# Shorter waits at the seams of a two-pass expert layer: rows counted at run time, tables and loads moved

## What is computed

```python
def _ln_c(v): return (v - v.mean(1)) / sqrt(v.var(1) + 1e-6)      # over channels, shortened
# attention in windows of 8 x 8 tokens
q, k, v = windows(wq @ xn + bq), windows(wk @ xn + bk), windows(wv @ xn + bv)
x = x + wo @ merge(softmax(q k^T / sqrt(128)) v) + bo             # xn = _ln_c(x)
# experts: E = 16, the two best of each token
t = to_tokens(x)
xt = _ln_t(t)
top_vals, top_idx = top_k(xt @ wg, 2)
w = softmax(top_vals)
for e in range(16):
    h = silu(xt @ w0[e]) * (xt @ w1[e])                           # 128 -> 256
    out = out + dense_w[..., e] * (h @ wo[e])                     # 256 -> 128
x = from_tokens(t + out)
```

## Time and profile before

| | us |
|---|---|
| median of 3 runs | 437.34 (437.17 to 438.48) |
| the profiled execution | 439.65 |
| its span, first to last instruction | 437.6 |

### The profile page before, as it was taken

How to read it: one execution, slowest core, us unless ns; L and a number is a source line. 1 busy time by engine, 2 the same in 40 slices (tenths; PEclk the granted TensorE clock), 3 DMA queues, 4 the chain that set the end, 5 groups by cost and what they waited for, 6 DMA issues and landing times.

```text
span 437.6 us, 9336 instructions
## 1 busy us (share of the span) xinstructions
PE 374.4 (86%) x2581; PEld 307.4 (70%) x2581; DVE 303.2 (69%) x1101; ACT 268.2 (61%) x778; POOL 234.7 (54%) x286
## 2 busy tenths in 40 slices
PE   4698887888876489999999999679999999999373
PEld 4476676666755348888888888458888888888242
DVE  4578999999986865766767667326767676676163
ACT  2688888887883136666666666336666666666100
POOL 7000055665575577776666666606666676666400
PEclk9999999999997558999999999969999999999886
DMA  7999999740110176777655532265454454421299
GB/s 231 365 350 197 160 152 149 223 149 26 39 51 31 49 158 161 200 210 203 178 140 141 141 117 86 99 175 162 141 145 131 127 152 133 140 64 49 99 351 348
DMA packets 56151, 68.07 MB, mean 156 GB/s; under 512 B 7588, under 2 KB 44328, under 8 KB 55800
## 3 DMA queue, kind: packets, MB, share of 16 engines
q1 hardware_dynamic: 45136, 43.13, 42.6%
q0 software_dynamic: 8368, 20.03, 13.3%
q10 hardware_dynamic: 2600, 4.33, 2.6%
HBM read 37.03 MB, written 36.65 MB: 168 GB/s over the span
## 4 chain that ended last, share of the span: by engine, by line
PE 62%; DVE 21%; DMA 7%; ACT 4%; SPq 3%; issue 2%; POOL 0%; POOLq 0%; DVEq 0%
PE bank L657 9%; PE bank L660 9%; PE bank L658 9%; PE bank L676 8%; PE bank L677 8%; PE bank L649 4%; PE bank L666 4%; PE bank L665 4%; DMA w_hi<-token_sums 3%; DMA w<-in_L_ffn_w 2%; DVE x_sb L1070 2%; DVE st L1016 2%; DVE st L1007 2%; SPq L345 2%; PE bank L492 2%
## 5 line engine op out<-in xcount | busy, mean ns | idle before, releaser
L1215 DVE SCALAR_TENSOR_TENSOR hid<-bank,late,sil 128x256 f32<-128x256 f32 x158 | 76.4, 484 | 73.6 <-ACT sil L841 72.4
L436 POOL DMA_INDIRECT token_sums<-late x79 | 76.5, 968 | 51.5 <-DVE late L1226 48.4
L841 ACT ACTIVATE sil<-bank,late 128x256 f32<-128x256 f32 x158 | 75.0, 475 | 46.0 <-PE bank L660 46.0
L432 POOL DMA_INDIRECT rows_second<-late x79 | 76.6, 970 | 35.9 <-DVE late L1224 30.7
L424 POOL DMA_INDIRECT rows_first<-rows,slot x64 | 63.5, 992 | 38.8 <-issue 16.8
L847 ACT COPY hT<-bank 128x256 f32<-128x256 f32 x158 | 59.1, 374 | 32.3 <-PE bank L666 31.3
L657 PE MATMUL bank<-w_hi,x_hi 128*128 x158 | 77.6, 491 | 1.1 <-ACT x_hi L836 1.1
L676 PEld LDWEIGHTS bank<-w_sb,hT 128*128 128x128 f32 x316 | 48.2, 190 | 29.2 <-issue 28.7
L660 PE MATMUL bank<-w_hi,x_lo 128*128 x158 | 64.3, 407 | 0.0
L676 PE MATMUL bank<-w_sb,hT 128*128 x316 | 61.8, 277 | 2.2 <-ACT hT L847 2.2
L658 PE MATMUL bank<-w,x_hi 128*128 x158 | 63.5, 402 | 0.0
(11 more groups left out here) (181 smaller groups left out, 663.3 us busy)
## 6 DMA issues: line engine op xcount, KB each, us to landing
late<-rows_second SPq DMA_DIRECT2D x79, 129.5 KB, 2.3
late<-rows_first SPq DMA_DIRECT2D x79, 66.5 KB, 2.5
w<-in_L_ffn_w SPq DMA_DIRECT2D x4, 1024.0 KB, 11.2
w_hi<-token_sums SPq DMA_DIRECT2D x16, 256.0 KB, 6.3
out<-x_sb ACTq DMA_DIRECT2D x16, 256.0 KB, 7.1
rows_second<-nobody_second SPq DMA_DIRECT2D x16, 129.5 KB
nobody_first<-late SPq DMA_DIRECT2D x1, 2061.5 KB, 21.4
x_sb<-in_x SPq DMA_DIRECT2D x1, 2048.0 KB, 13.6
```

The lines of the kernel that those rows point to most:

```text
L432: pool.indirect_dma_start(out=xs2_dram, out_offset=bass.IndirectOffsetOnAxis(ap=xg[:, u, 0:1].bitcast(I32), axis=0), in_=xg[:, u, TOK:TOK ...
L436: pool.indirect_dma_start(out=s_dram, out_offset=bass.IndirectOffsetOnAxis(ap=xg[:, u, TOK:TOK + 1].bitcast(I32), axis=0), in_=xg[:, u, YA ...
L841: act.activation(sil[:, t % 2, :], bank[2 + t % 2][:, 0:M], ACT.Silu, scale=xg[:, t % XRING, RS:RS + 1]).then_inc(sil_ok, 1)
L1215: dve.scalar_tensor_tensor(out=hid[:, t % 2, :], in0=bank[2 + t % 2][:, M:2 * M], scalar=xg[:, t % XRING, RS:RS + 1], in1=sil[:, t % 2, :] ...
```

## The change

- **Waits for tiles with rows.** TensorE adds up how many tiles of each pass have rows (`T_ALL`, one product in `tiles_upto`), VectorE turns this to a count of landings for each slot (`left_i`, three operations in `tables`), and SP reads 16 numbers (`rows_left`) and waits for these alone, ahead of pass two and ahead of the loads of the sums. The wait for all scatters comes behind these loads.
- **Room.** The sums are loaded to `rows`, `xn` and a buffer of five chunks, no longer over `w_hi`. XRING goes from 20 to 16.
- **Weights at the start** come in four quarters (EP = 4), with four experts in period 0 instead of five.
- **TensorE** does `full_ends` in period 16 behind `last_rows`, `full_rows` behind the last `last_rows`, and `tiles_upto` and `tiles_rows` one tile later. **VectorE** does `ends` and `tile_counts` behind the first tile's product, `tiles_done` and `tables` one tile later.
- **GpSimd** holds the scatters of a batch back to TensorE's and ScalarE's later periods, two by two, and does the next batch's counts ahead of the last two.

```diff
-XRING = 20
+XRING = 16
-SPLIT0 = 5
+EP = SPLIT0 = 4
...
+        def s_in(n):
+            return (s_in1[:, n, :, :] if n < TAIL1 else xn[:, n - TAIL1, :, :] if n < TAIL1 + 2
+                    else s_in2[:, n - TAIL1 - 2, :, :])
...
-            for k in range(2):
-                es = slice(k * (E // 2), (k + 1) * (E // 2))
+            for k in range(E // EP):
+                es = slice(k * EP, (k + 1) * EP)
...
+            def rows_left(k):
+                sp.wait_ge(left_ok, 1)
+                left = []
+                for u in range(XRING):
...
+                    left.append(sp.value_load(left_i[0:1, 2, k, u:u + 1], min_val=least, max_val=most))
+                for u in range(XRING):
+                    sp.wait_ge(y_out[u], left[u])
...
                     sp.wait_ge(pads2_in, (E + 1) * 16)
-                    for w in range(XRING):
-                        sp.wait_ge(y_out[w], len(range(w, TL, XRING)) * 16)
+                    rows_left(0)
...
+            rows_left(1)
+            s_v = s_dram[0:N, :].rearrange("(n p j) d -> p n j d", j=TPC, p=P)
+            for n in range(NCH):
+                sp.dma_start(s_in(n), s_v[:, n, :, :]).then_inc(s_got[n], 16)
             for u in range(XRING):
                 sp.wait_ge(y_out[u], len(range(u, TILES, XRING)) * 16)
...
                 for j in range(TB):
+                    n = min(2 * m + 7 + j // 4, NCH)
+                    if j % 2 == 0 and m == LAST:
+                        past(pool, xhi_ok, j // 2)
+                    elif j % 4 == 2:
+                        pool.wait_ge(q_ok, n)
+                    elif j == 4:
+                        pool.wait_ge(xnt_ok, n)
+                    if j == 6:
+                        counts(m + 1)
                     pool.indirect_dma_start(
...
                 token_rows(i + 2)
...
+                if i == NCH:
+                    full_ends()
...
-                if i == NCH - 1:
-                    full_ends()
             new_rows(NCH - 1)
+            last_rows(NCH - 1)
             full_rows()
-            last_rows(NCH - 1)
...
                 pe.wait_ge(nt_ok, 1)
+                pe.matmul(T_ALL, ones_f[0:E, 0:32], nt_f[:, 0, :], start=True, stop=True)
...
-                    if t == 0:
+                    if t == 1:
                         tiles_upto()
-                    if t == 1:
+                    if t == 2:
                         tiles_rows()
...
             place(LAST)
-            ends()
-            tile_counts()
...
                     if t == 0:
+                        ends()
+                        tile_counts()
+                    if t == 1:
                         tiles_done()
-                    if t == 1:
+                    if t == 2:
                         tables()
```

More of the change, by code:

```diff
@@ L181, in emit @@
         T_END, T_SUM, T_UPTO = SP_[0:32, 0:2 * E], SP_[0:E, 2 * E:2 * E + 2], SP_[0:E, 2 * E + 2:2 * E + 4]
+        T_ALL = SP_[0:32, 2 * E + 4 + 4 * TL:2 * E + 6 + 4 * TL]
         T_ROW = SP_[0:32, 2 * E + 4:2 * E + 4 + 4 * TL]
         wqk_in = sem("wqk_in"); wov_in = sem("wov_in"); b_in = sem("b_in"); wg_in = sem("wg_in")
[L186 removed]
+        e_in = [sem(f"e_in{k}") for k in range(E // EP)]; e2_in = sem("e2_in"); e_hi = sem("e_hi"); e_lo = sem("e_lo")
         x_in = [sem(f"x_in{n}") for n in range(6)]
@@ L394, in _, with counts @@
             make(pool.memset(gap0[:, :], float(CAPT)))
+            count(left_k[:, :, :], [[TL, 2], [-1, XRING]], base_=XRING - 1)
             assert made.count == CONST1
             count(iota_r[:, :, :], [[0, 2], [P, TL]])
-            for m in range(NBAT):
-                b = m % RB
+            def counts(m):
                 if m < LAST:
@@ L415, in _ @@
                                        ALU.add).then_inc(carry_ok, 1)
+            counts(0)
+            for m in range(NBAT):
+                b = m % RB
                 past(pool, sc[b], m // RB * TB * 16)
@@ L712, in _ @@
                 for j in range(TPC):
-                    mm = pe.transpose(bank[n % 2][:, tiles[j]], s_in[:, n, j, :], ident[:, :])
+                    mm = pe.transpose(bank[n % 2][:, tiles[j]], s_in(n)[:, j, :], ident[:, :])
                 mm.then_inc(ot_ps, 1)
@@ L1172, in tables @@
                 dve.wait_ge(row_ps, 1)
+                left = then(dve.tensor_tensor(left_i[:, 0, :, :], T_ALL[0:1, :].unsqueeze(2).to_broadcast([1, 2, XRING]),
+                                              left_k[:, :, :], ALU.add))
                 rest = slice(FULL, 2 * TL)
@@ L1180, in tables @@
                                   float(E - 1), float(2 * D), ALU.min, ALU.mult).then_inc(expert_ok, 1)
+                after(left)
+                left = then(dve.tensor_scalar(left_i[:, 1, :, :], left_i[:, 0, :, :], 4, None, ALU.logical_shift_right))
+                after(left)
+                dve.tensor_scalar(left_i[:, 2, :, :], left_i[:, 1, :, :], 4, None,
+                                  ALU.logical_shift_left).then_inc(left_ok, 1)
             dve.wait_ge(made_s, CONST0)
```

20 lines of the change are left out of this document (12 added, 8 removed).

## The result

| | before | after |
|---|---|---|
| median of the runs, us | 437.25 (436.90 to 438.48, 4 runs) | 412.91 (412.21 to 413.39, 4 runs) |
| span of the profiled execution, us | 437.6 | 410.8 |
| its mean granted clock of TensorE | 0.936 | 0.972 |

The ratio is 0.943, 95% interval 0.9409 to 0.9452: 24.3 us less by the medians, where 24.5 was forecast. The two profiled spans are 26.8 apart, 2.5 more.

What follows compares the result with a forecast made beforehand. The prediction saw TensorE gapless inside the passes, with time to win at five seams where it stands still. Terms 2.0 + 4.0 - 0.2 + 0 + 7.7 + 11.0 = 24.5 off 437.34 gave 412.8 us, range 408.8 to 419.5.

Steps and rivals of the forecast that it cites:

- Start, 2.0 forecast: Kernel start: weights in quarters bring the queries 2.3 us earlier, less 0.3 for the fifth cast; gain 2.0 us.
- End of the attention stage, 4.0: End of attention: two VectorE waits go (2.45 us) and TensorE's clock stays up (0.94 and 0.57); gain 4.0 us.
- Tables, -0.2: Tile tables one tile later: same work, still at the slow clock, plus a few small operations; cost 0.2 us.
- Scatters held back, 0: GpSimd's scatters during the attention stage: GpSimd is off the chain there, so holding them back gains zero.
- Ring of 16, 0: Start of pass one: tile 16 lands with 2.9 us to spare despite the smaller ring; zero effect.
- Seam, 7.7: Between the two tile passes: TensorE resumes 5.8 us earlier and full clock adds 1.9; gain 7.7 us.
- End, 11.0: Kernel end: loads of the sums start 11.3 us earlier, beside the empty tiles; gain 11.0 us.
- Slow clock in the tail: Rival: slow clock at the seam and in the final transposes; gain only 17.2, time 420.1 us; chance 0.07.
- numbers read slowly: Rival: SP's number reads at seam and end take 1.2 us each, making both late; 423.4 us; chance 0.05.
- the short ring: Rival: at the start of pass one tiles 16 to 23 come 1 to 5 us late; about 415.8 us; chance 0.10.
- the pacing by the ring: Rival: the ring of 16 paces every tile, slower than before; 39 us lost, 452 us; chance 0.01.
- only the waits go, not the clock: Rival: at attention's end and the seam only waiting is saved, clock stays low; 21.1 gained, 416.3 us; chance 0.15.

Runs made afterwards that it cites:

- halves: Changed kernel with the expert weights loaded in two halves and five experts in period 0 again: 414.98 us, ratio 0.9495.
- tables_early: Changed kernel with the tile tables' products and counts back in their old, earlier places: 414.30 us, ratio 0.9467.
- ring16: Kernel before the change with XRING cut from 20 to 16 and nothing else: 438.30 us, ratio 1.0005.
- warm: Changed kernel plus 41 unused identity transposes where TensorE waits between about 132 and 150 us: 411.55 us, ratio 0.9402.
- before_again: Kernel before the change, unchanged, timed and profiled a second time: 437.48 us, ratio 0.9995.
- after_again: Changed kernel, unaltered, timed and profiled once more: 412.63 us, ratio 0.9437.
- seam_all: Changed kernel with the full wait for all of pass one's scatters back at the start of pass two: 421.67 us, ratio 0.9644.
- reads_twice: Changed kernel meant to load each of the 16 numbers twice; the second loads were not in the program that ran: 413.47 us, ratio 0.9451.
- full_ends_early: Changed kernel with full_ends back at the end of period 15 and full_rows ahead of the last last_rows: 415.91 us, ratio 0.9502.
- unpaced: Changed kernel with a batch's eight scatters issued at once again, the next batch's counts behind them: 414.87 us, ratio 0.9483.
- tail_all: Changed kernel with the full wait for all scatters back ahead of the loads of the sums: 423.30 us, ratio 0.9668.
- warm2: Changed kernel with more unused transposes: 44 for the earlier 24, six for the last four, nine at the start: 409.16 us, ratio 0.935.

## Why the prediction was right, point by point

- **Start, 2.0 forecast.** The queries moved by 2.25 us (2.3 forecast), and undoing it costs 2.2. The 0.3 us of the fifth cast are there in halves, though period 1 to 15 as a whole became 0.2 us shorter. VectorE's period 1 came 2.7 us earlier in the mean of three profiles, but 22.3 to 24.1 in single ones: there TensorE's clock comes back at one of several moments, which the forecast did not have.
- **End of the attention stage, 4.0.** 3.8 in the profiles. That the clock stays up to period 16 was right; undone it costs 3.0 in its stage. The 0.57 us of the ranks did not come: at that point the clock had fallen again (at 135.3 us, and at 135.3 and 137.8 in the other two profiles), and period 16 to tile 0 stayed at 14.2.
- **Tables, -0.2.** The wrong sign. Undoing the move costs 1.5 us. The step that failed is "that is the same one tile later, still at the slow clock": in after the product of 316 columns took 0.71 us, since the clock was back by then, and 1.25 in tables_early. That explains 0.5; the rest is the later return of the clock (160.6 for 156). Whether the order of the products shifts it, and why, is not shown.
- **Scatters held back, 0.** In its own stage 0.2; by the medians 2.1. Open, as said at the run.
- **Ring of 16, 0.** Right: ring16 shows no change and no wait. In after, tile 0's scatter starts at 164.12, 15.7 us behind TensorE's first tile (its transpose at 148.47), where the forecast counted 17, and TensorE waits for no tile's rows from 149 to 200 us there either.
- **Seam, 7.7.** 8.1 in the profiles, and the split of the forecast (5.8 of waiting, 1.9 of clock) is 6.2 and 1.9. TensorE's own order is next late, as said: the wait for a load is gone. It was right with a wrong duration in it: SyncE's first load came 3.2 us behind the last scatter that counts (264.65 to 267.85), where 2.66 from a quieter moment had been taken. The slack was large enough. The numbers cost 0.59 us each, for the 0.55 that was taken.
- **End, 11.0.** 10.2. The loads start 11.3 us earlier, exactly the step. The term that was too small is the share of the wires that the empty tiles take: the phase is 1.0 us longer (26.4 for 25.3), and the forecast had 0.3. The clock did not fall while TensorE worked. The Trainium skill (TensorE: Matmul & The Clock Gate, Part 4: PE-mode transpose) has it that transposes don't count as busy; the trace disagrees, with 1.00 from 392.6 to 404.4 us and, in warm, over the 24 transposes ahead of 142.5.
- **The rivals.** Slow clock in the tail, numbers read slowly, the short ring and the pacing by the ring did not happen. Of "only the waits go, not the clock" one piece did: the clock fell a period later. The sum of this rival is 0.2 too large, as its terms make 20.9 and not 21.1.
- **The sum.** 24.5 forecast, 24.3 by the medians, 25.5 by three profiles each. The 1.2 us between the last two are the choice of executions: the profiled ones of before took 439.65, 436.21 and 438.29 us, 0.8 above the median in the mean, and those of after 412.58, 412.63 and 411.84, 0.45 below 412.8. The span of 437.6 was 0.3 above the median of the device times, but its execution took 439.65, 2.3 above; taking the gains off the median was right. That the sum met the number to 0.2 us is in part luck: down the table the forecast missed by 0.9 us in the first two rows together, -0.2, 0.7 in the next two, 0.4 and -0.8, and errors of both signs cancel. The parts undone one by one cost 28.3 (2.2, 3.1, 1.5, 2.1, 8.9, 10.5), more than the whole. Each of these differences is good to about 1 us, and a single edit can go with another return of the clock, as the 1.6 us in tile 0 to 78 of tables_early show; how much of the excess comes from either is not shown.

## What to carry to other kernels

Where an engine's wait is removed, look at what its clock did in and behind that wait: of the seam's 8.1 us 1.9 were clock, and 3.6 us more came from filling the waits that are left with products that nobody reads. Before a term is read from one trace, profile the same kernel twice; here the spans lay 3.4 us apart, and 2.5 of them lay in one place, where the clock came back. Before a run is taken as evidence, look in its trace whether the edit is there: the doubled loads were not. A wait on all of a queue is worth replacing by one on the part that carries data, but the rest of the queue still takes its share of the wires.

## What the runs showed of the hardware

- TensorE's clock came back at different moments in executions of the same work. Behind tile 0's first product it returned after 3.5 to 4.1 us (before_again, after_again, halves, seam_all, warm), 6.3 to 6.7 (after, reads_twice, full_ends_early, unpaced, tail_all) or 9.3 to 10.2 (before, ring16, tables_early). Tile 0 to 78 took 117.0 to 117.8 us in the first five, 118.5 to 118.7 in the next and 119.4 to 119.9 in the last. Executions of before in one comparison with a mean clock of 0.944 took 435.1 to 437.0 us, those with 0.929 took 438.4 to 438.9.
- At the start the views show 1.00 where the trace has no record of the granted clock. The record opens at 15.85 us in after and at 21.75 in after_again. In after_again the 16 logits products at 16.51 take 1.18 us, in after 0.73; period 1 starts at 24.06 and at 22.31.

```profile
16.51 1.18 PE L542 MATMUL bank<-xnT,q_sb 128*64 128x64 f32 x16 [0.84 <-ACT q_sb L815]
```

- Products whose result nobody reads (fp32 transposes of 128x128, 0.11 to 0.12 us each in the rows of 44 and 24) held the clock at 1.00 in warm2 and cost nothing where they fit the wait.
- A load of one number with its two checks kept SyncE for 0.59 us (after), 0.27 of them the load.
- Loads and stores together moved 404 to 407 GB/s for 11 us in the last phase.
- A scatter's landing took 2.66 us on quiet wires. With loads beside it, it took longer: those of before from 262 to 284 us took 2.4, 2.8 and 3.4 (shortest, median, longest), and at the seam of after, from 257 to 274 us:

```profile
DMA to landing us min/median/max: 2.4/3.5/4.4
```
